# Four-layer graph network kernel: attention's first tile prepared during the first projections, whose input is laid out transposed

## The reference

```python
# layer 0: attention with 8 heads of 64 keys, masked by adj
keys, queries, values = einsum('nj,hjk->hnk', x, Wks), ...   # Wqs, Wvs
atts = queries @ keys.T / 8 - 1e16 * (1 - adj)
out  = einsum('hqm,hmk,hko->qo', softmax(atts), values, Wo)
x = layernorm(x + out)
# layer 1: x = layernorm(x + relu((adj @ x) @ W.T + b))
# layer 2: h = x @ edge_w; e = softmax(where(adj > 0, h @ h.T, -9e15))
#          att = softmax(x @ node_w, axis=0) * e
#          x = layernorm(x + (adj * att) @ (x @ weight) + b)
# layer 3: a = adj + I, d = rowsum(a) ** -0.5
#          x = layernorm(x + relu((d * a * d) @ x @ W.T + b))
```

## Time and profile before

| | us |
|---|---|
| median of 3 runs | 2541.1 |
| lowest and highest | 2539.39, 2542.22 |
| profiled execution | 2541.41, its span 2539.6 |

### The profile page before, as it was taken

One profiled execution on the slowest core, in us unless ns is written; L12 is line 12 of the kernel. 1 busy time (PEld: TensorE's weight loads), 2 busy tenths in 40 slices (PEclk: granted clock), 3 DMA queues, 4 the chain that ended last, 5 costly groups with the idle time before them and its releaser, 6 DMA issues. The chain is left out here.

```text
span 2539.6 us, 67049 instructions
## 1 busy us (share of the span) xinstructions
PE 2424.1 (95%) x24988; PEld 1557.7 (61%) x24988; DVE 1545.9 (61%) x3013; ACT 1364.0 (54%) x2036; POOL 1148.7 (45%) x971
## 2 busy tenths in 40 slices
PE   7997999999999999999879997999999999979998
PEld 6885777777777777777634443774444555534443
DVE  4435998898888898888632222555555566633222
ACT  3335888888888888888623221324434444323222
POOL 0005888888888888888601232001111113310323
PEclk9998999999999999999989999999999999989999
DMA  3216999999999999999743654215666779733664
GB/s 130 65 62 129 183 195 185 188 193 181 190 193 178 187 193 184 191 188 185 123 137 118 213 199 158 100 37 138 175 183 181 203 207 233 178 128 101 211 213 140
DMA packets 783644, 417.41 MB, mean 164 GB/s; under 512 B 691296, under 2 KB 717664, under 8 KB 774496
## 3 DMA queue, kind: packets, MB, share of 16 engines
q1 hardware_dynamic: 783456, 414.62, 70.7%
HBM read 203.55 MB, written 40.84 MB: 96 GB/s over the span
## 5 line engine op out<-in xcount | busy, mean ns | idle before, releaser
L806 DVE CUSTOM_DVE_ANT_0 att_scores<-att_slots,att_adj 128x1024 f32<-128x1024 f32 x528 | 575.7, 1091 | 41.6 <-POOL att_part_low L627 14.5
L627 POOL TENSOR_TENSOR att_part_low<-att_scores,att_part_high 128x1024 f16<-128x1024 f32 x352 | 574.8, 1651 | 12.0 <-ACT att_part_high L790 1.1
L751 ACT ACTIVATE att_scores<-att_scores,att_nmax 128x1024 f32<-128x1024 f32 x528 | 552.4, 1047 | 28.2 <-DVE att_lifted L817 26.0
L672 PE MATMUL att_slots<-l_kk,att_q 128*128 128x512 f16 x2112 | 466.5, 356 | 15.5 <-DMA att_q<-q_rows 8.9
L1345 PE MATMUL a_ps<-l_y,a_adj 128*128 128x512 f16 x1936 | 421.2, 381 | 9.0 <-DVE a_adj L1359 4.7
L825 DVE TENSOR_TENSOR att_near_low<-att_ps_t,att_near_high 128x512 f16<-128x512 f32 x528 | 316.4, 599 | 37.6 <-ACT att_near_high L760 35.9
L760 ACT ACTIVATE att_near_high<-att_ps_t 128x512 f16<-128x512 f32 x528 | 258.2, 524 | 150.0 <-PE att_ps_t L682 137.3
L1345 PEld LDWEIGHTS a_ps<-l_y,a_adj 128*128 128x128 f16 x1936 | 190.0, 98 | 240.1 <-DVE a_adj L1359 5.2
L672 PEld LDWEIGHTS att_slots<-l_kk,att_q 128*128 128x128 f16 x2112 | 195.2, 98 | 173.4 <-DVE att_least L806 24.9
L1090 PE MATMUL edge_ps_o<-l_sup,edge_pt_high 128*128 128x512 f16 x968 | 287.9, 379 | 1.7 <-DMA edge_pt_low<-edge_part_low 1.7
L1330 ACT ACTIVATE a_adj<-l_adj 128x2816 f16<-128x2816 f32 x44 | 112.0, 2549 | 291.1 <-DMA l_adj<-in_adj_cols 271.1
(11 more groups left out here) (152 smaller groups left out, 3863.2 us busy)
## 6 DMA issues: line engine op xcount, KB each, us to landing
l_adj<-in_adj_cols SPq DMA_DIRECT2D x44, 1408.0 KB, 6.1
l_adj_tiles<-in_adj SPq DMA_DIRECT2D x22, 1354.0 KB, 6.1
att_adj<-in_adj SPq DMA_DIRECT2D x66, 384.0 KB, 4.2
p_x_in<-x SPq DMA_DIRECT2D x66, 256.0 KB, 2.6
att_q<-q_rows SPq DMA_DIRECT2D x44, 256.0 KB, 3.8
a_xres<-x SPq DMA_DIRECT2D x44, 256.0 KB, 2.8
p_x_in<-in_x SPq DMA_DIRECT2D x22, 256.0 KB, 2.7
q_rows<-l0w_q_halves SPq DMA_DIRECT2D x22, 256.0 KB, 2.1
```

The costliest lines, as they stand in the source:

```text
L627: nc.gpsimd.tensor_tensor(out=part[1][:, v, lo:lo + width], in0=sc[:, v, lo:lo + width], in1=part[0][:, v, lo:lo + width], op=ALU.subtract ...
L672: mm = nc.tensor.matmul(slots[:, slot, z:z + w], q[:, u, h % 2, a, h // 2, :], kk[:, h, lo + z:lo + z + w], start=a == 0, stop=a == 1)
L751: nc.scalar.activation(sc[:, v, lo:lo + width], sc[:, v, lo:lo + width], ACT.Exp, bias=nmax[:, v:v + 1], scale=-1.0).then_inc(exp_done, 1)
L806: nc.vector.tensor_tensor_reduce(out=sc[:, v, lo:lo + width], in0=slots[:, (NC * h + c) % 2, 0:width], in1=adj[:, u, lo:lo + width], scale ...
```

## The change

The host also passes `x_cols`: for each row tile of x its transpose, in blocks, so that a load of a tile (256 KB) brings it as `turn` would have left it. The first `project` (`columns=True`) loads from it and makes no transposes; `ps_t` is then `x_in`, so both splits read SBUF, and `turned` is `xt_low`. In all `project` calls, x tile 1 is loaded after the first two own weight loads, no longer after all.

With `ahead`, the first `project` also does what attention did at its start: POOL clears the pads and sets the ones column in `vv` and makes `off_diag`; SP loads the first row tile of the adjacency in one DMA behind the broadcasts; POOL does bias and diagonal in one operation each; SP loads the queries of tile 0 after the x loads. `adj`, `q` and `off_diag` are allocated outside of both blocks. Attention starts without these steps, its semaphore counts are one tile lower, and PE and DVE skip their waits for the first tile. PE waits for two memsets of the scores' pads.

```diff
@@ -112,8 +112,8 @@
 
-    def load(self, sp):
-        for (src, stage, _h, _l), loaded in zip(self.parts, self.loaded):
+    def load(self, sp, which=slice(None)):
+        for (src, stage, _h, _l), loaded in zip(self.parts[which], self.loaded[which]):
             sp.dma_start(stage, src).then_inc(loaded, 16)
@@ -169,12 +169,12 @@
         junk = s.sb("junk", [P, D])
-        ps_t = s.ps("ps_t", [P, 2, BANK])
+        ps_t = x_in if columns else s.ps("ps_t", [P, 2, BANK])
         ps_job = [s.ps(f"ps_job{n}", [P, 2, BANK]) for n in range(len(jobs))]
         x_loaded = [s.sem(f"x_loaded{u}") for u in range(2)]
-        turned = s.sem("turned")
         xt_high = s.sem("xt_high")
         xt_low = s.sem("xt_low")
+        turned = xt_low if columns else s.sem("turned")
         made = s.sem("made")
@@ -191,7 +191,29 @@
             dy_ready = s.sem("dy_ready")
+        if ahead is not None:
+            adj, q, q_rows, adj_rows, vv, off_diag = ahead
+            first_adj, first_q, first_bias = s.sem("first_adj"), s.sem("first_q"), s.sem("first_bias")
+            ones_ready = s.sem("ones_ready")
         block = ctx.enter_context(nc.Block())
+
+        if ahead is not None:
+            @block.gpsimd
+            def _(pool):
+                nc.gpsimd.memset(adj[:, :, N:NP], -BIG).then_inc(first_bias, 1)
+                nc.gpsimd.memset(vv[:, 0:T - 1, :, P:P + 1], 1.0).then_inc(ones_ready, 1)
+                nc.gpsimd.memset(vv[:, T - 1, :, P:P + 1], 0.0).then_inc(ones_ready, 1)
+                pool.wait_ge(ones_ready, 2)
+                nc.gpsimd.memset(vv[0:LAST, T - 1, :, P:P + 1], 1.0).then_inc(ones_ready, 1)
+                nc.gpsimd.tensor_scalar(out=off_diag[:, :], in0=ident[:, :], scalar1=-1.0, scalar2=1.0, op0=ALU.mult,
+                                        op1=ALU.add).then_inc(first_bias, 1)
+                pool.wait_ge(first_adj, 16)
+                nc.gpsimd.tensor_scalar(out=adj[:, 0, 0:N], in0=adj[:, 0, 0:N], scalar1=BIG, scalar2=-BIG,
+                                        op0=ALU.mult, op1=ALU.add).then_inc(first_bias, 1)
+                pool.wait_ge(first_bias, 3)
+                nc.gpsimd.tensor_tensor(out=adj[:, 0, 0:P], in0=adj[:, 0, 0:P], in1=off_diag[:, :], op=ALU.mult) \
+                    .then_inc(first_bias, 1)
+                pool.wait_ge(first_bias, 4)
 
@@ -211,8 +233,9 @@
                         sp.wait_ge(scored, 2 * m + u - 1)
-                sp.dma_start(x_in[:, u, :], x_rows[bass.ds((2 * m + u) * P, P), :]) \
-                    .then_inc(x_loaded[u], 16)
+                src = x_rows[bass.ds((2 * m + u), 1), :, :].rearrange("o p n -> (o p) n") if columns \
+                    else x_rows[bass.ds((2 * m + u) * P, P), :]
+                sp.dma_start(x_in[:, u, :], src).then_inc(x_loaded[u], 16)
 
@@ -227,18 +250,28 @@
             load(0, 0)
-            own.load(sp)
+            own.load(sp, slice(0, 2))
             load(0, 1)
+            own.load(sp, slice(2, None))
             late_w.load(sp)
...
                 sp.dma_start(dst, src).then_inc(prefetched, 16)
+            if ahead is not None:
+                sp.dma_start(adj[:, 0, 0:N], adj_rows[0:P, :]).then_inc(first_adj, 16)
             pairs(sp, 4, T, late)
+            if ahead is not None:
+                sp.wait_ge(kept_stored[0], 16)
+                for e in range(2):
+                    sp.dma_start(q[e * KD:e * KD + KD, 0, :, :, :, :].rearrange("p e a j r -> p e (a j r)"),
+                                 q_rows[0:P, :].rearrange("(e p) n -> p e n", e=2)).then_inc(first_q, 16)
             keep(T // 2 - 1, 0)
...
                 sp.wait_ge(prefetched, 16 * len(prefetch))
+            if ahead is not None:
+                sp.wait_ge(first_q, 32)
             if kept is not None:
@@ -246,6 +279,8 @@
             def turn(m, u):
+                if columns:
+                    return
                 pe.wait_ge(x_loaded[u], 16 * m + 16)
@@ -285,7 +320,10 @@
             def split(m, u):
-                act.wait_ge(turned, 2 * m + u + 1)
+                if columns:
+                    act.wait_ge(x_loaded[u], 16 * m + 16)
+                else:
+                    act.wait_ge(turned, 2 * m + u + 1)
                 if not (isinstance(m, int) and m == 0):
@@ -462,10 +500,7 @@
         s = Scope(nc, ctx, "att", layer)
-        adj = s.sb("adj", [P, 2, NP])
-        off_diag = s.sb("off_diag", [P, P])
         xres = s.sb("xres", [P, D])
-        q = s.sb("q", [P, 2, 2, 2, J, P], F16)
         sc = s.sb("scores", [P, 2, NP])
@@ -483,8 +518,7 @@
         xres_loaded = s.sem("xres_loaded")
-        pad_clear, ones_ready = s.sem("pad_clear"), s.sem("ones_ready")
-        off_diag_ready = s.sem("off_diag_ready")
+        pad_clear = s.sem("pad_clear")
         bias_ready = s.sem("bias_ready")
@@ -588,35 +622,25 @@
 
-            for half in range(2):
-                load_q(0, 0, half)
-            for n in range(len(ADJ_PARTS)):
-                load_adj(0, 0, n)
             all_steps(sp, step)
...
         def _(pool):
-            nc.gpsimd.memset(adj[:, :, N:NP], -BIG).then_inc(pad_clear, 1)
-            nc.gpsimd.memset(sc[:, :, N:NP], 0.0).then_inc(tail_clear, 1)
-            nc.gpsimd.memset(vv[:, 0:T - 1, :, P:P + 1], 1.0).then_inc(ones_ready, 1)
-            nc.gpsimd.memset(vv[:, T - 1, :, P:P + 1], 0.0).then_inc(ones_ready, 1)
-            pool.wait_ge(ones_ready, 2)
-            nc.gpsimd.memset(vv[0:LAST, T - 1, :, P:P + 1], 1.0).then_inc(ones_ready, 1)
+            nc.gpsimd.memset(sc[:, 0, N:NP], 0.0).then_inc(pad_clear, 1)
+            nc.gpsimd.memset(sc[:, 1, N:NP], 0.0).then_inc(tail_clear, 1)
             norm.exponent(nc, pool)
-            nc.gpsimd.tensor_scalar(out=off_diag[:, :], in0=ident[:, :], scalar1=-1.0, scalar2=1.0, op0=ALU.mult,
-                                    op1=ALU.add).then_inc(off_diag_ready, 1)
 
...
                 lo, width = ADJ_PARTS[n]
-                wait_apart(pool, adj_loaded[n][u], 16 * m + 16, pad_clear)
+                wait_apart(pool, adj_loaded[n][u], 16 * (m + u), pad_clear)
                 nc.gpsimd.tensor_scalar(out=adj[:, u, lo:lo + width], in0=adj[:, u, lo:lo + width], scalar1=BIG,
...
                 t = 2 * m + u
-                wait_apart(pool, bias_ready, len(ADJ_PARTS) * (t + 1), pad_clear)
+                wait_apart(pool, bias_ready, len(ADJ_PARTS) * t, pad_clear)
                 part_of = adj[:, u, bass.ds(t * P, P)]
@@ -653,10 +677,6 @@
 
-            for n in range(len(ADJ_PARTS)):
-                bias(0, 0, n)
-            pool.wait_ge(off_diag_ready, 1)
-            diagonal(0, 0)
             all_steps(pool, step)
@@ -718,8 +738,8 @@
                 if on(0):
-                    if h == 0:
-                        pe.wait_ge(q_loaded[u], 32 * (m + 1))
+                    if h == 0 and not is_tile(m, u, 0):
+                        pe.wait_ge(q_loaded[u], 32 * (m + u))
                     scores(i, u, h, 0)
@@ -844,8 +864,8 @@
                 if on(0):
-                    if h == 0:
-                        dve.wait_ge(diag_ready, t + 1)
+                    if h == 0 and not is_tile(m, u, 0):
+                        dve.wait_ge(diag_ready, t)
                     mask(i, u, h, 0)
@@ -1420,6 +1440,8 @@
             output = parts(s, "wo")
+            bias, q = s.sb("bias", [P, 2, NP]), s.sb("q", [P, 2, 2, 2, J, P], F16)
+            off_diag = s.sb("off_diag", [P, P])
             with ExitStack() as inner:
@@ -1440,12 +1462,13 @@
 
-                project(nc, s, "p0", x, ident, [(wk, *key), (wv, *value), (wq, *query)],
+                project(nc, s, "p0", x_cols, ident, [(wk, *key), (wv, *value), (wq, *query)],
                         [("cols", *key, keys), ("rows", *value, values), ("cols", *query, queries)],
...
                         prefetch=[(row[:, :], vector.broadcast_to([P, D])) for row, vector in
-                                  ((b1_row, b1), (b2_row, b2), (b3_row, b3), (node_row, node_w))])
-            attention(nc, s, x, x1, q_rows, adj, kk, vv, output, ident)
+                                  ((b1_row, b1), (b2_row, b2), (b3_row, b3), (node_row, node_w))], columns=True,
+                        ahead=(bias, q, q_rows, adj, vv, off_diag))
+            attention(nc, s, x, x1, q_rows, adj, kk, vv, output, ident, bias, q, off_diag)
 
@@ -1499,7 +1522,8 @@
     arrays = {
-        "x": padded(x, (NP, D)), "adj": padded(adj, (NP, N)), "adj_cols": cols,
+        "x": padded(x, (NP, D)), "x_cols": padded(x, (NP, D)).reshape(T, P, J, P).transpose(0, 3, 2, 1).reshape(T, P, D),
+        "adj": padded(adj, (NP, N)), "adj_cols": cols,
         "wk": heads(L0_gnn_Wks), "wq": heads(L0_gnn_Wqs), "wv": heads(L0_gnn_Wvs),
```

More of the change, by code:

```diff
@@ L152, in project @@
 def project(nc, layer, tag, x_rows, ident, weights, jobs, score=None, degrees=None, kept=None, later=(),
-            prefetch=()):
+            prefetch=(), columns=False, ahead=None):
     with ExitStack() as ctx:
@@ L454, with attention @@
```

(9 more changed lines are left out.)

## The result

The changed kernel takes 2520.13 us (median of 4 runs, 2518.34 to 2522.3); the kernel before, beside it, 2541.31. The ratio is 0.9918, with an interval of 0.9901 to 0.9935: 21 us faster, where 26 were forecast.

The account below looks back on a forecast made before the run. PE (TensorE), busy for 95% of the span, was taken to bound the kernel. Terms of 4.4 + 8.8 + 1.9 + 8.7 + 0.4 + 1.9 = 26.1 us off the median 2541.1 gave 2515.0 us, range 2510.5 to 2521.0.

Parts of the forecast that it names:

- bound of 1.4: First projection, x tile 4: a new PE wait of 1.4 us should the adjacency load take 5.5 us.
- Start: First projection's start: PE's first product at 10.79 us against 15.38; 4.4 us won, bounds 4.1 and 4.6.
- 0.45 us for the slow clock: First projection's start: up to 0.9 us more of products go at half rate, 0.45 us lost.
- Transposes: First projection: 20 turns of 0.44 us leave PE, 8.8 us won; splits reading SBUF cost nothing.
- The hole at tile 4: First projection: PE's 1.89 us wait for x tile 4, queued behind four broadcast loads, goes.
- rival of a late tile 4: First projection: adjacency load delays x tile 4 and POOL's bias falls beside DVE's split; 2518 us, chance 0.08.
- 0.6 us of slack: First projection: x tile 4's splits end near 43.8 us, PE wants them at 44.4.
- Handover: From first projection to attention: first mask near 2.45 us after the block's start against 11.17; 8.7 us won.
- rival of a clock that has not yet fallen: Handover to attention: PE's clock still full, head 0's pieces run at full rate; 2513.5 us, chance 0.05.
- After the first mask: Attention's third score piece: an earlier clock rise shortens it and part of DVE's waits; 0.4 us, bounds −0.4 and 1.6.
- Layer 2's start: Start of `p2`: x tile 1 ahead of the last two weight loads; 1.9 us won, bounds 0 and 3.
- slower rival: Attention: new SBUF places for `adj` and `q` make each of 176 heads cost more; 2550 us, chance 0.03.

## Why the prediction was right, and where it was not

The forecast was 2515.0 us with a range of 2510.5 to 2521.0; 2520.13 lies in it, 5.1 above the forecast. That it does is luck in part: tile 4 went 1.7 us beyond its bound of 1.4, edge attention had no term at all, and a handover that came out 0.8 us better took some of it back.

*Start: forecast 4.4, measured 3.7.* The first product came 4.56 us earlier. But products of 128 columns were at the slow pace until about 16 us (0.31 us at 15.79, 0.22 later), and tile 0's queries were written out at 21.47 instead of 25.20. I had 0.45 us for the slow clock; it cost about 0.9. The start also scatters by more than this error: in the other kernels with the new input or order, but without transposes of the identity, tile 0's queries were out between 19.87 and 22.89.

*Transposes: right.* 7.95 us a tile as forecast, and the splits from SBUF (0.62 us on ACT, 0.69 on DVE when undisturbed) cost no time.

*The hole at tile 4: the step that failed.* 1.9 us were to be won, and a wait of 3.08 is there: 3.1 us less than forecast. Two terms were mis-sized. The first is the load: I carried over 8.4 us from issue to use and added 3.5 for the adjacency at 384 KB per us. It took 14.7 us. The 8.4 held, since behind the broadcasts alone it was 8.6; the adjacency's term is the one that failed, with about 6.1 us instead of 3.5. Its rate wasn't the error (394 GB/s from 38 to 42 is what I had taken). By the times of landing in the trace, the queries' store and x tile 5, issued at 38.86 and 39.42, were in by 46.50 and 47.09, right behind x tile 4 (45.82), so they shared the engines with it, and my sum had no term for them. How the 2.6 us divide between them and the broadcasts, whose last one landed at 40.50, isn't shown. The kernel with the adjacency late and the one with the broadcasts late show from both sides that the wait needs both: no wait in either. The second is the contention, which the sum put at nothing: about 0.9 of the 3.08, by the kernel with the bias held back. My rival of a late tile 4, at 0.08, had both halves of the mechanism; its time (2518) was 2 us short of the median. It deserved a good part of the chance, since 0.6 us of slack stood on a sum of parts that were never seen together.

*Handover: forecast 8.7, measured 9.5.* The block's start, PE's start and the mask came as worked out. The 0.8 us are the rival of a clock that has not yet fallen, in part: full at PE's start, it fell at about 197.0. In the adjacency-late kernel it was the same (first eight products 2.22 us), while with the bias held back, with the late broadcasts and in the change run again they took 3.01 to 3.15 us after the same idle time of 4.35 us, and the mask came 2.4 to 2.5 us into the block, as forecast. So the 0.8 us belong to the run and not to the change, and the four timed runs may hold both cases. The Trainium skill, TensorE: Matmul & The Clock Gate, Part 1, says, of the clock's rise, that the point of change shifts from run to run. The traces show the same of its fall, with 2.19 and 3.15 us for the same eight products in two runs of the changed kernel.

*After the first mask: 0.4 forecast, nothing measured.* The third piece waited 1.03 us as before.

*Layer 2's start: forecast 1.9, measured 2.0.* Right, by the mechanism named. The size is less sure than it looks: over all traces `p2` to edge is 138.25 to 139.69 us with the old order and 137.03 to 137.76 with the new one, about 1.5 us apart.

*Not in the sum: edge attention, +2.2 us (up to +5 in other kernels).* I had said that the rest runs behind it in sequence and carries the gain to the end. It did, but for the last tile, where a wait of 1.7 us became one of 2.0 and pulled the clock down. That the wait and this fall cost the time is shown by the last transposes put ahead of the store: 516.36 us. Why the combined kernels always land on the worse side while each single part leaves 518, isn't settled; the code of that block is the same, and only the offset of the engines among each other moves, by the 0.3 to 0.9 us between DVE's splits and `x_out` above.

*The rest.* From the first mask to `p1` the kernels took 1056.2 to 1063.5 us, with no relation that I could find to what was changed in them. The 1.3 us lost there are within that scatter, and so are the smaller differences of the other stretches. The slower rival (heads that cost more) fell: 200 us of attention hold 3078 and 3055 products, as before.

The sum, by what was measured: 3.7 + 8.8 + 1.9 − 3.1 + 9.5 + 2.0 = 22.8, less the 3.1 us from unchanged blocks, is 19.7 of 19.8. The terms are of one pair of executions, and each can differ by about 1 us in another.

The preparation ahead, then, pays only where the projection has room for it. Beside the transposed input alone it wins some 9 us at the handover and gives 4.9 back ahead of it (block start 190.66 against 195.53; 1.6 of these lie at the start, where the two runs differ too); alone it gives back 6.3 of 8.7, and the time shows no gain.

## What to carry to other kernels

A load that is moved ahead of a block pays where it is taken out and costs where it is put in: work out the queue it joins with all that lies ahead of the engine's next load and all that is issued before that load lands, and put what the engine needs next in front of it. Before and after a wait look at PE's clock; a wait that grows by 0.3 us can cost 2 when the clock falls behind it, anywhere later in the kernel. Test the parts alone and together: here the parts share one gain, and one of them shows none by itself.

## What the runs showed of the hardware

*DVE's split and POOL's bias: one waits for the other.* In seven traces DVE's split with two inputs in SBUF started during POOL's bias and took 1.55 to 1.69 us instead of 0.69. It always ended 0.53 to 0.55 us after the bias did: 54.49 + 2.45 = 56.94 and 55.93 + 1.55 = 57.48; 45.23 + 2.45 = 47.68 and 46.59 + 1.63 = 48.22. That is the time of a split that stands until POOL is done and then runs. The other way round, POOL's `x_out` of 2.08 us took 3.12, 4.17, 4.18 and 4.78 us where it met DVE's three splits in edge attention. The Trainium skill, SBUF — State Buffer, section SBUF: two separate sides, says that the port pair of DVE and GpSimd is an exclusive lock, held by whoever starts first for the whole instruction. By that rule the price is the rest of the other's pass, not a share of the rate; the traces of the bias agree, with the 0.54 us at the end of each.

The rule doesn't give every overlap. In the changed kernel DVE's three splits started 0.18 us behind `x_out`:

```profile
2185.76 2.08 POOL L468 TENSOR_SCALAR edge_x_out<-all_b_row,edge_mv,edge_rstd 128x512 f32<-128x512 f32 x1 [0.20 <-POOL edge_rstd L459]
...
2185.94 3.56 DVE L1239 SCALAR_TENSOR_TENSOR edge_part_low<-edge_scores,edge_part_high 128x1024 f16<-128x1024 f32 x3 [2.43 <-ACT edge_part_high L1143]
```

They take 3.12 us when nothing holds them, as in the adjacency-late kernel. Had they stood until `x_out` was done, at 2187.84, they would have ended near 2191.0; they ended at 2189.50, only 0.4 us longer than undisturbed. So most of the 2.08 us of `x_out` didn't hold DVE. Whether POOL works on SBUF for only a part of that span, or doesn't keep the port for all of it, isn't shown.

*Broadcasts are slow loads.* While four loads of a row to 128 partitions were under way, the queue moved 134 to 171 GB/s in windows of 2 and 4 us (e.g. 34 to 38 in the changed kernel); in the windows behind, the adjacency and x ran at 394 to 426.

*A clock can fall while PE works.* In the changed kernel PE started at 195.99 at full clock after 4.36 us idle, and the clock fell at about 197.0 amid its products. With transposes in the idle stretch, which left 1.50 us of it, the clock stayed full there; at the start of the same kernel, 2.73 us of idle time behind 40 transposes were followed by a fall about 1 us into PE's work.
